# Pre-norm linear-attention block with a matrix layer on one core: the normalisation of x's columns moves from GpSimd to VectorE, and the passage to the second half is reordered

## The chip, the cores and the metric

The kernel runs on one core of one Trainium2 chip. The metric is the device time of the whole program in microseconds, lower is better. The engines are TensorE (PE in the profile; PEld is its loading of weights), VectorE (DVE), ScalarE (ACT), GpSimd (POOL) and SyncE (SP). SP only issues DMAs here; ACT issues some too.

## The reference

```python
def reference(x, Wq, Wk, Wv, Wo, Wa, ba, CB, SCB, bias):   # x: (4, 2048, 512) fp32
    n = layernorm(x)                       # over the 512 columns, eps 1e-5
    q, k, v = n @ Wq, n @ Wk, n @ Wv       # 512 -> 1024 = 16 heads of 64
    q, k = elu(q) + 1, elu(k) + 1
    a = sigmoid(n @ Wa + ba + 2)           # one decay per head and token
    # per head, over the tokens of a sequence:
    #   S = a*S + k v^T,  z = a*z + k,  out = (q S) / (q z + 1e-6)
    x = x + out @ Wo                       # 1024 -> 512
    n2 = layernorm(x)
    return x + (n2 @ CB.T) * (SCB / 127) + bias
```

## The kernel before, in words

The 8192 tokens are cut into NC = 64 chunks of 128. Matrix products are done in three passes (high part by high part, high by low, low by high) of numbers split in two: ScalarE makes the high part with a copy (`..._hi`), VectorE subtracts it for the low part (`..._lo`).

**First half** (`step`, i from -1 to NC + 1, on every engine; chunks are taken two by two, `pair`, with b = i % 2). TensorE makes k and v of a chunk (`unit`, 12 matmuls of 512 columns each) and q of two chunks together (`q_unit`, 24 matmuls of 256 columns), and between these, at the head of each step, the small matmuls of the attention: `transposes` of k, `carried` (q by the state), `delta` (k by v), `within` (scores by v), `scores`. `transposes` waits at its head for VectorE's results of the step before (`M`, `qs`, `S_mid`, the weighted v, all of k and q). The first steps (to 1 on TensorE, to 3 on the others) and the last ones are written out; between them each engine runs a loop.

**x's columns.** The first product needs the normalised x with its 512 columns on the partitions. SP loads a pair's transposed x (`xT_in`, 128 x 4 x 256 numbers). The statistics are per token, so they lie on partitions (`moments`, 128 x 2 chunks x 2), and have to be laid out along the free dimension of all partitions: `store_norm` (L508) writes `moments` to `norm_rows` in HBM, and `spread_norm` (L513) loads it into all 128 partitions of `bias_b`. In the even step GpSimd first makes the inverse deviation for the next pair (L627), waits for `xT_loaded` and `norm_loaded`, and subtracts the mean (L644) and multiplies by the inverse deviation (L648), in four instructions of 128 x 256 each. After this ScalarE (`x_hi`) and VectorE (`x_lo`, L905) split the columns in the odd step. `norm_rows` is [C, 4], so the four numbers of a token are one piece of 16 bytes.

**SP's order** in an even step (L520 to 564): `store_norm`; a wait for TensorE's `num_ready[0]` of the step before; `spread_norm`, which waits until the store has landed; four loads of decays (`abc`, `spread_decays`, L458); `store_rows(1)` (L422, four DMAs); four loads of products (`pbc`, L467); `store_rows(0)`. Every SP instruction waits in this order.

**VectorE's order** in an even step, from `elu_k(1, 0)` on (L1152 to 1190): `elu_k(1)`, `normalised(0)` (den, rden, num_sb, attn), `decay_matrix(1)` (a scan, L1109), `weighted_v(1)` (L1012), `elu_q(2)`, `decay_matrix(0)`, `elu_q(3)`, `elu_k(0)`, `carried_on`. `elu_k(0)` is the last thing for which TensorE's next `transposes` waits; it needs ScalarE's relu and exp of the last k unit.

**Second half** (`step2`): per chunk a product of the attention's rows with Wo (`output_product`, 24 matmuls into DS), `residual` (add x, statistics), the inverse deviation on GpSimd, `residual_normal`, a transpose, the split (`fT_hi`, `fT_lo`), the matrix layer (`ffn_product`, 12 matmuls into NUM), and the sum that is stored.

**The passage** between them: SP loads the matrix layer's weights, `scale` and `bias` (`ffn_weights`, L409), GpSimd multiplies the four weight tiles by `scale` (L655), ScalarE and VectorE split them (`ffn_weights_hi` L692, `ffn_weights_lo` L941). The columns of chunk 0 are turned by TensorE (`turn`, L1566) and split by `turned_hi` (L847) and `turned_lo` (L1210). VectorE ends step NC + 1 with `residual(1)`, `residual_normal(1)`, `rows_lo(3)` and `normalised(1)` of the last chunk, whose transpose waits until the attention rows stored before it have left `attn`; then in step2(1) come `residual(2)` with the bias and the deviation, and `ffn_weights_lo`; in step2(2) `residual_normal(2)`, `turned_lo`, the transpose of chunk 1, `rows_lo(4)` and `residual(3)`; in step2(3) `fT_lo` of chunk 1 and `residual(4)`. TensorE's first `ffn_product` (L1592) waits for all four low weight tiles and for `turned_lo`, behind the output product of chunk 2.

```python
510                     sp.wait_ge(rstd_ready, pairs[1])
511                     sp.dma_start(norm_rows, moments[:, :, :].rearrange("p s a -> p (s a)")).then_inc(norm_stored, 16)
...
515                     sp.wait_ge(norm_stored, p16[0])
516                     wait(sp, xT_normal, pairs[-1])
517                     sp.dma_start(bias_b[:, :], norm_rows.rearrange("(q c) m -> q (c m)", q=1).broadcast_to([128, 4 * C]))\
```

## Time and profile before

| | |
|---|---|
| median of 3 runs | 1965.36 us (1963.75 to 1965.54) |
| the profiled execution, its own time | 1965.75 us |
| its span | 1964.0 us |
| mean granted TensorE clock | 0.998 |
| PE busy | 1939.4 us, 99% |
| DVE busy | 1645.7 us, 84% |
| ACT busy | 687.1 us, 35% |
| POOL busy | 389.6 us, 20% |
| steps of the first half | 24.8 to about 1431 us |
| second half | about 1431 us to the end |

A line of a timeline or a page gives the engine, the line of the kernel (L1109), the operation, the tensor written <- the tensors read, and in brackets the idle time of the engine just before it with what ended it. SPq and ACTq are the issuing of DMAs. "Idle" of an engine other than TensorE costs nothing in itself. 1.75 us of the profiled execution lie outside its span.

### The profile page before, as it was taken

To read this page: it belongs to the slowest core of one execution; us is meant where nothing else is said; L and a number is where in the kernel's file an instruction comes from. 1 tells how busy PE (TensorE), PEld (TensorE's weight loads), DVE (VectorE), ACT (ScalarE), POOL (GpSimd) and SP (SyncE) were. 2 spreads that over 40 slices of the span, in tenths; PEclk is the share of its full clock that TensorE was granted. 3 is DMA by queue.
4 is the path that set the end of the run, shared out by engine and by line. 5 is a ranking of instruction groups with operands and counts; after the bars stand their busy time and mean duration, and the time that the engine had idled before them with its cause. 6 is when DMAs were issued, how large, how long until landed. Compare 5 with 4: busy or idle time off the path is not lost.

```text
span 1964.0 us, 69099 instructions
## 1 busy us (share of the span) xinstructions
PE 1939.4 (99%) x26926; PEld 1690.8 (86%) x26926; DVE 1645.7 (84%) x2918; ACT 687.1 (35%) x1288; POOL 389.6 (20%) x368
## 2 busy tenths in 40 slices
PE   8999999999999999999999999999989999999999
PEld 7888888898888888988888888888878888888887
DVE  8788888888888888888888888888787777777776
ACT  5334334333433343344333433343422222222221
POOL 3222222232222222332222223222010000000000
PEclk9999999999999999999999999999999999999999
DMA  6343443444443444444344444445476666666665
GB/s 217 89 94 96 99 115 94 110 106 104 100 97 98 105 105 108 104 104 105 97 98 102 108 101 107 105 108 128 98 164 163 161 161 161 161 160 160 161 161 117
DMA packets 596067, 237.40 MB, mean 121 GB/s; under 512 B 432064, under 2 KB 546240, under 8 KB 596032
## 3 DMA queue, kind: packets, MB, share of 16 engines
q1 hardware_dynamic: 560896, 204.94, 43.9%
q10 hardware_dynamic: 35136, 32.00, 5.7%
q8 instruction: 21, 0.34, 0.1%
q14 instruction: 14, 0.11, 0.0%
HBM read 168.59 MB, written 51.97 MB: 112 GB/s over the span
## 4 chain that ended last, share of the span: by engine, by line
PE 95%; DVE 2%; issue 1%; DMA 1%; SPq 1%; POOL 0%; ACT 0%; POOLq 0%; DVEq 0%
PE G L1325 54%; PE DS L1283 17%; PE NUM L1283 9%; PE NUM L1394 4%; PE SC L1447 3%; PE DS L1426 3%; PE NUM L1408 3%; PE SC L1273 2%; PE DS L1467 1%; DVE w_lo L912 0%; DMA attn_cols<-attn 0%; SPq L429 0%; DMA norm_rows<-moments 0%; DMA abc<-decay_rows 0%; DVE D L1109 0%
## 5 line engine op out<-in xcount | busy, mean ns | idle before, releaser
L1325 PE MATMUL G<-w_hi,xT_hi 128*128 128x512 f32 x1024 | 406.9, 397 | 0.4 <-DVE w_lo L912 0.4
L1325 PE MATMUL G<-w_lo,xT_hi 128*128 128x512 f32 x1024 | 399.8, 390 | 0.0
L1325 PE MATMUL G<-w_hi,xT_lo 128*128 128x512 f32 x1024 | 398.7, 389 | 0.0
L734 ACT ACTIVATE relu_t<-G 128x512 f32<-128x512 f32 x256 | 153.4, 599 | 451.9 <-PE G L1325 449.9
L1325 PE MATMUL G<-xT_hi,w_hi 128*128 128x256 f32 x1024 | 290.2, 283 | 0.2 <-DVE w_lo L912 0.2
L1325 PE MATMUL G<-xT_lo,w_hi 128*128 128x256 f32 x1024 | 289.8, 283 | 0.0
L1325 PE MATMUL G<-xT_hi,w_lo 128*128 128x256 f32 x1024 | 289.7, 283 | 0.0
L1325 PEld LDWEIGHTS G<-w_hi,xT_hi 128*128 128x128 f32 x1024 | 192.4, 188 | 42.2 <-issue 0.6
L1325 PEld LDWEIGHTS G<-w_hi,xT_lo 128*128 128x128 f32 x1024 | 192.3, 188 | 41.4
L1325 PEld LDWEIGHTS G<-w_lo,xT_hi 128*128 128x128 f32 x1024 | 192.6, 188 | 35.5
L702 ACT ACTIVATE w_hi<-at_rows 128x512 fp32r<-128x512 f32 x128 | 73.8, 624 | 383.7 <-PE DS L1283 365.9
L1325 PEld LDWEIGHTS G<-xT_hi,w_hi 128*128 128x128 f32 x1024 | 196.3, 192 | 3.9 <-DVE w_lo L912 0.7
L1283 PE MATMUL DS<-w_hi 128*128 128x512 f32 x512 | 199.5, 390 | 0.0
L1283 PE MATMUL DS<-w_hi,w_lo 128*128 128x512 f32 x512 | 199.2, 389 | 0.0
L1283 PE MATMUL DS<-w_lo,w_hi 128*128 128x512 f32 x512 | 199.2, 389 | 0.0
L644 POOL TENSOR_TENSOR xT_in<-xT_in,bias_b 128x256 f32<-128x256 f32 x124 | 140.4, 1163 | 295.3 <-DMA bias_b<-norm_rows 295.3
L1325 PEld LDWEIGHTS G<-xT_hi,w_lo 128*128 128x128 f32 x1024 | 196.3, 192 | 2.4
L1325 PEld LDWEIGHTS G<-xT_lo,w_hi 128*128 128x128 f32 x1024 | 196.3, 192 | 0.0
L648 POOL TENSOR_TENSOR xT_in<-xT_in,bias_b 128x256 f32<-128x256 f32 x124 | 182.0, 1495 | 2.4
L1109 DVE TENSOR_TENSOR_SCAN D<-abc,eye 128x512 f32<-128x512 f32 x128 | 175.0, 1367 | 0.5 <-DMA abc<-decay_rows 0.5
L629 POOL TENSOR_TENSOR moments<-vareps,minus_half 128x2 f32<-128x2 f32 x32 | 22.5, 702 | 716.3 <-DVE vareps L894 716.3
L735 ACT ACTIVATE exp_t<-G 128x512 f32<-128x512 f32 x256 | 151.7, 593 | 0.0
(137 smaller groups left out, 3609.0 us busy)
## 6 DMA issues: line engine op xcount, KB each, us to landing
abc<-decay_rows SPq DMA_DIRECT2D x256, 128.0 KB, 3.2
pbc<-product_rows SPq DMA_DIRECT2D x256, 128.0 KB, 3.1
attn_cols<-attn SPq DMA_DIRECT2D x512, 64.0 KB, 2.2
at_rows<-attn_cols ACTq DMA_DIRECT2D x244, 128.0 KB, 2.8
xt<-in_x SPq DMA_DIRECT2D x64, 256.0 KB, 3.1
x_in<-in_x SPq DMA_DIRECT2D x64, 256.0 KB, 3.0
out_rows<-xt SPq DMA_DIRECT2D x64, 256.0 KB, 3.0
xT_in<-in_xT SPq DMA_DIRECT2D x31, 512.0 KB, 4.4
```

Source lines behind the costliest of these rows:

```text
L644: made = pool.tensor_tensor(x4[:, kt, :, :], x4[:, kt, :, :], norm_b[:, 0, :, :], ALU.subtract)
L648: made = pool.tensor_tensor(x4[:, kt, :, :], x4[:, kt, :, :], norm_b[:, 1, :, :], ALU.mult)
L702: act.activation(turned_out(oT_hi[b], r), turned_in(b, r), ACT.Copy).then_inc(oT_hi_ready[r], 1)
L734: act.activation(relu_t[buffer][:, :], bank[:, :], ACT.Relu)
L735: act.activation(exp_t[buffer][:, :], bank[:, :], ACT.Exp).then_inc(ready, 1)
L1109: nc.vector.tensor_tensor_scan(D[:, hs(r), :].rearrange("p h c -> p (h c)"), abc[:, HH * L * r:HH * L * (r + 1)], eye8[:, :, :].rearrange( ...
L1283: made = nc.tensor.matmul(to, a[:, kt, :], w[:, kt, :], start=(kt == 0 and n == 0), stop=(kt == tiles_k - 1 and n == 2))
L1325: made = nc.tensor.matmul(to, lhs, rhs, start=(n == 0), stop=(n == len(passes) - 1))
L1394: made = nc.tensor.matmul(num_of(a, e, j), qs[ps, GH * r + j, L * a:L * a + L], (S_mid if a else S[o])[ps, GH * r + j, :], start=(j == 0), ...
L1408: made = nc.tensor.matmul(num_of(a, e, j), M[ps, r, 2 * j + e, :], v1[o][ps, HH * r + 2 * j + e, :], start=False, stop=(j == GH - 1))
L1426: made = nc.tensor.matmul(DS[64 * e:64 * e + 64, U * a + E * j:U * a + E * j + E], k[ps, DH * h:DH * h + DH], vw[ps, h, :], start=True, st ...
L1447: made = nc.tensor.matmul(SC[64 * a:64 * a + 64, at:at + L], kT[ps, GH * r + j, ts], qT[ps, GH * r + j, C * (b ^ r) + L * a:C * (b ^ r) + ...
```

## The change

- `norm_rows` becomes [4, C]: the means of the even chunk, its inverse deviations, and those of the odd chunk are four runs of 128 numbers. The store writes 512 single numbers of 4 bytes; the load still gives each partition 512 numbers, and `norm_b` is now contiguous in the token.
- `store_norm` stands behind the wait for `num_ready[0]`; `spread_norm` behind the four loads of decays.
- GpSimd's eight instructions per pair are gone (its inverse deviation stays); VectorE does them as two of 128 x 1024: the subtraction ahead of `elu_q(2)`, the multiplication behind `decay_matrix(0)` and ahead of `elu_q(3)`, both in the even step.
- Passage: `turned_hi`/`turned_lo` of chunk 0 move to step2(1), ahead of the weights; the weights' splits are cut into two and two (step2(1) and step2(2)); GpSimd's inverse deviation of chunk 1 goes between the second and the third weight multiplication; TensorE's first `ffn_product` waits for each weight tile by itself; VectorE's `normalised(1)` of the last chunk and SP's `store_rows(1)` of it move to the end of step2(3).

```diff
-    norm_rows = nc.dram_tensor("norm_rows", [C, 4], fp32).ap()
+    norm_rows = nc.dram_tensor("norm_rows", [4, C], fp32).ap()
...
-        norm_b = bias_b[:, :].rearrange("p (c s a) -> p a s c", s=2, a=2)
+        norm_b = bias_b[:, :].rearrange("p (s a c) -> p a s c", s=2, a=2)
+        x_tiles = xT_in[:, :, :].rearrange("p k (s c) -> p k s c", s=2)
...
                 def store_norm():
-                    sp.dma_start(norm_rows, moments[:, :, :].rearrange("p s a -> p (s a)")).then_inc(norm_stored, 16)
+                    sp.dma_start(norm_rows.rearrange("m c -> c m"), moments[:, :, :].rearrange("p s a -> p (s a)"),
+                                 allow_slow_non_contiguous=True).then_inc(norm_stored, 16)
...
                 gates = b == 1 and exists(i + 1)
-                if b == 0 and exists(i + 2):
-                    store_norm()
                 if b == 0 and exists(i):
                     wait(sp, num_ready[0], one[-1])
                 if b == 0 and exists(i + 2):
-                    spread_norm()
+                    store_norm()
                 if exists(i):
                     spread_decays(1, this_pair, b)
                 if b == 0 and exists(i + 1):
                     spread_decays(0, this_pair, 1)
+                if b == 0 and exists(i + 2):
+                    spread_norm()
...
-                if exists(i - 2):
+                if exists(i - 2) and not (isinstance(i, int) and i == NC + 1):
                     store_rows(1, i - 2, one[-2])
...   (SP, end of step2)
+                if isinstance(i, int) and i == 3:
+                    store_rows(1, NC - 1, NC)
...   (GpSimd, step)
-                    inverse_deviation(pairs[1])
-                    pool.wait_ge(xT_loaded, p16[0])
-                    pool.wait_ge(norm_loaded, p16[0])
-                    for kt in range(KT):
-                        made = pool.tensor_tensor(x4[:, kt, :, :], x4[:, kt, :, :], norm_b[:, 0, :, :], ALU.subtract)
-                    made.then_inc(xT_centred, 1)
-                    pool.wait_ge(xT_centred, pairs[0])
-                    for kt in range(KT):
-                        made = pool.tensor_tensor(x4[:, kt, :, :], x4[:, kt, :, :], norm_b[:, 1, :, :], ALU.mult)
-                    made.then_inc(xT_normal, 1)
+                    inverse_deviation(counts(pool, pair, 1, (1,))[1])
                 if isinstance(i, int) and i == NC:
...
                     for kt in range(KT):
+                        if kt == 2:
+                            inverse_deviation2(2)
                         pool.tensor_tensor(raw_wf[kt], raw_wf[kt], scale, ALU.mult).then_inc(wf_scaled, 1)
...   (ScalarE, step2)
-                if isinstance(i, int) and i == 2:
-                    turned_hi(1, 0)
                 if exists(i + 1):
                     rows_hi(r64[1], one[-1], 1 - b)
+                if isinstance(i, int) and i == 2:
+                    ffn_weights_hi(range(2, KT))
...
                 if isinstance(i, int) and i == 1:
-                    ffn_weights_hi()
+                    turned_hi(1, 0)
+                    ffn_weights_hi(range(2))
...   (VectorE, step)
+                def centred_columns():
+                    dve.wait_ge(xT_loaded, x16[0])
+                    dve.wait_ge(norm_loaded, x16[0])
+                    nc.vector.tensor_tensor(x_tiles, x_tiles, over_tiles(0), ALU.subtract).then_inc(xT_centred, 1)
+                def normal_columns():
+                    dve.wait_ge(xT_centred, pairs[0])
+                    nc.vector.tensor_tensor(x_tiles, x_tiles, over_tiles(1), ALU.mult).then_inc(xT_normal, 1)
...
                 elif exists(i + 1):
+                    if exists(i + 2):
+                        centred_columns()
                     elu_q(2, 1)
                     decay_matrix(0)
+                    if exists(i + 2):
+                        normal_columns()
                     elu_q(3, 0)
...   (VectorE, end of step NC + 1)
                     rows_lo(3, 0)
-                    normalised(1)
...   (VectorE, step2)
-                if isinstance(i, int) and i == 2:
-                    turned_lo(1, 0)
...   (behind the transpose of step2)
+                if isinstance(i, int) and i == 2:
+                    ffn_weights_lo(range(2, KT))
...   (end of step2)
-                if isinstance(i, int) and i == 1:
-                    ffn_weights_lo()
+                if opening:
+                    turned_lo(1, 0)
+                    ffn_weights_lo(range(2))
+                if isinstance(i, int) and i == 3:
+                    normalised(1, NC, 64 * (NC - 1))
...   (TensorE, step2)
                 if isinstance(i, int) and i == 2:
-                    pe.wait_ge(wf_lo_ready, KT)
-                if exists(i - 2):
+                    pe.wait_ge(num_copied[1], NC)
+                    pe.wait_ge(fT_lo_ready, 1)
+                    for kt in range(KT):
+                        pe.wait_ge(wf_lo_ready, kt + 1)
+                        made = passes(F[0], (fT_hi[0], fT_lo[0]), (wf_hi, wf_lo), range(kt, kt + 1), KT)
+                    made.then_inc(F_ready, 1)
+                elif exists(i - 2):
```

`over_tiles(a)` is `norm_b[:, a:a + 1, :, :].broadcast_to([128, KT, 2, C])`: the same 256 numbers for each of the four column tiles. `normalised(1)` in steps 2 to NC is the same as before; it only takes its counts as arguments.

## Rows read from the trace of the kernel before

**Rows 1.** The page, part 1, busy time of each engine.
```profile
PE 1939.4 (99%) x26926; PEld 1690.8 (86%) x26926; DVE 1645.7 (84%) x2918; ACT 687.1 (35%) x1288; POOL 389.6 (20%) x368
```
**Rows 2.** Waits of PE: what it waited for, us in total, times, longest.
```profile
PE NUM L1394 <- issue: 6.8, 5, 2.2
...
PE NUM L1283 <- DVE w_lo L1213: 4.4, 1, 4.4
PE SC L1273 <- DVE k L996: 2.0, 1, 2.0
```
**Rows 3.** Windows: busy us (instructions) of each engine, then granted clock, DMA share, GB/s.
```profile
50.00:52.00 2.00, 2.00 (x98) 2.00 (x93) 0.95 (x3) 0.00 (x0) 0.00 (x0) 0.60 0.00 0
...
1452.00:1453.00 1.00, 1.00 (x4) 0.81 (x3) 1.00 (x3) 0.00 (x0) 0.00 (x0) 0.50 0.41 119
```
**Rows 4.** Timeline of DVE in an even step, GpSimd busy from 784.18 on.
```profile
784.53 1.12 DVE L996 SCALAR_TENSOR_TENSOR k<-exp_t,relu_t 128x512 f32<-128x512 f32 x1 [0.15 <-ACT exp_t L735]
...
789.78 1.13 DVE L1012 TENSOR_TENSOR vw<-v,D 128x520 f32<-128x520 f32 x1
...
793.93 1.28 DVE L1003 SCALAR_TENSOR_TENSOR qT<-exp_t,relu_t 128x512 f32<-128x512 f32 x1
795.75 0.69 DVE L996 SCALAR_TENSOR_TENSOR k<-exp_t,relu_t 128x512 f32<-128x512 f32 x1 [0.54 <-ACT exp_t L735]
```
**Rows 5.** Timeline of DVE in the odd step before, same instructions, GpSimd idle.
```profile
766.30 0.69 DVE L996 SCALAR_TENSOR_TENSOR k<-exp_t,relu_t 128x512 f32<-128x512 f32 x1
...
768.77 1.18 DVE L1109 TENSOR_TENSOR_SCAN D<-abc,eye 128x512 f32<-128x512 f32 x1
770.05 0.70 DVE L1012 TENSOR_TENSOR vw<-v,D 128x520 f32<-128x520 f32 x1
```
**Rows 6.** Timeline of SP's DMA issues in the even step of rows 4.
```profile
780.49 0.33 SPq L517 DMA_DIRECT2D bias_b<-norm_rows  x1
781.02 2.62 SPq L463 DMA_DIRECT2D abc<-decay_rows  x4
```
**Rows 7.** DMA issues: tensors, queue, count, KB each, median us to landing.
```profile
bias_b<-norm_rows SPq DMA_DIRECT2D x31, 256.0 KB, 3.2
...
norm_rows<-moments SPq DMA_DIRECT2D x31, 2.0 KB, 2.2
```
**Rows 8.** The row stores of 700 to 900 us by themselves (72 of them).
```profile
DMA to landing us min/median/max: 2.1/2.2/4.3
```
**Rows 9.** Opening, DVE timeline: from the scaled q to the last k.
```profile
37.22 1.31 DVE L1064 TENSOR_TENSOR qs<-qT,pbc 128x512 f32<-128x512 f32 x1
...
45.78 1.34 DVE L996 SCALAR_TENSOR_TENSOR k<-exp_t,relu_t 128x512 f32<-128x512 f32 x1
```
**Rows 10.** Opening and a later step, chain of waits: start us, us, what.
```profile
49.24 1.99 PE SC L1447 x64
...
96.72 1.02 PE SC L1447 x64
```
**Rows 11.** Passage, timeline of DVE.
```profile
1444.65 0.71 DVE L1081 STREAM_TRANSPOSE attn<-num_sb 128x512 f32<-128x512 f32 x1 [3.75 <-DMA attn_cols<-attn]
1445.28 0.65 DVE L958 TENSOR_TENSOR relu_t<-DS,x_in 128x512 f32<-128x512 f32 x1
...
1452.15 1.24 DVE L950 TENSOR_TENSOR w_lo<-at_rows,w_hi 128x512 fp32r<-128x512 f32 x2
...
1459.13 0.70 DVE L1231 TENSOR_TENSOR w_lo<-kT,w_hi 128x512 fp32r<-128x512 f32 x1
```
**Rows 12.** Passage, timeline of POOL.
```profile
1437.41 0.66 POOL L633 TENSOR_TENSOR rstd<-vareps,minus_half 128x1 f32<-128x1 f32 x1 [73.57 <-DVE vareps L970]
1441.39 2.56 POOL L655 TENSOR_TENSOR abc<-abc,eye 128x512 f32<-128x512 f32 x2 [3.32 <-DMA qT<-in_CBT]
```
**Rows 13.** Passage, chain of waits: the first two matrix-layer products.
```profile
1451.35 4.47 PE NUM L1283 x12
...
1461.27 2.72 PE NUM L1283 x12
```

More of the change, by code:

```diff
@@ L1146, in step @@
                     rows_lo(2, 1)
-                    normalised(1)
+                    normalised(1, one[-2], a64[-3])
                 if exists(i):
@@ L1154, in step @@
                 if exists(i - 1) and not last:
-                    normalised(0)
+                    normalised(0, one[-1], a64[-2])
                 if exists(i):
@@ L1159, in step @@
                 if last:
-                    normalised(0)
+                    normalised(0, one[-1], a64[-2])
                 if isinstance(i, int) and i == NC - 2:
```

59 lines of the change are left out of this document (29 added, 30 removed).

## The prediction, made before the changed kernel was run

> **What bounds the kernel now.** Read the page's busy times first: TensorE is busy for 1939.4 of 1964.0 us, VectorE for 84% [rows 1]. So little over 24 us of the span can be won unless TensorE's work changes, and the diff changes none of it. VectorE and GpSimd matter only where TensorE waits for them. The waits of PE come next [rows 2]: 4.4 us once for a low part on VectorE (the first matrix-layer product, in the passage), 2.0 us once for VectorE's k (in the opening), and 6.8 us in five places where it waits for nothing that the profile shows. The change can touch the first two. Third, the granted clock behind them: 0.60 from 50 to 52 us, behind the wait of the opening, and 0.50 behind that of the passage [rows 3], where 1.0 is 2.4 GHz and 0.5 is 1.2 GHz. Each of the two idle stretches is therefore paid twice, once as a wait and once in matmuls at the low clock. Last, the timelines of VectorE, SP and GpSimd, for what the moved work meets.
>
> **Part 1, the normalisation in the steady steps (31 pairs).** Removed are eight GpSimd instructions; no one but ScalarE, VectorE and TensorE in the next step waits for their result, so that alone is worth nothing. What they cost is seen on VectorE. From `elu_k(1)` to the start of `weighted_v(1)` takes 789.78 - 784.53 = 5.25 us with GpSimd busy [rows 4] and 770.05 - 766.30 = 3.75 us in the odd step with GpSimd idle [rows 5]: 1.5 us lost. From there to the end of `elu_q(3)` takes 5.43 us (to 795.21) [rows 4], for which the undisturbed prices are about 0.61 for each 512-column operation and 1.28 for the scan (768.77 to 770.05 [rows 5]), so 0.61 + 0.61 + 1.28 + 0.61 = 3.1: 2.3 us lost. Together some 3.8 us a pair come back.
>
> Beside this row stands a rule of the Trainium skill, "SBUF — State Buffer", the sections on engine ports: a VectorE instruction with two SBUF inputs and a GpSimd instruction that reads SBUF exclude each other for the whole instruction. The rows agree in sign (0.69 against 1.12 us for the same k), not in a full block; the sum goes by the rows.
>
> Added on VectorE are two instructions of 128 x 1024. Nothing of this size is in the trace. It is bounded by two of 512 back to back: 1.24 us for a pair of `rows_lo` [rows 11] and 1.40 for two at the length of `vw` with its start and end [rows 5]. I take 1.22, the spacing of instructions that follow each other, as one long instruction saves one start; so 2.4 us a pair (2.4 to 2.8) come in and 3.8 go out. VectorE then reaches `elu_k(0)` at 784.53 + 3.75 + 0.61 + 1.22 + 0.61 + 1.28 + 1.22 + 0.61 = 793.8, while ScalarE hands the k over only at 795.75, where VectorE already waited 0.54 us before [rows 4]. So 1.9 us of room stand ahead of the instruction on which TensorE depends. The steady steps stay as they are: priced at nothing, hidden behind TensorE's q, k and v matmuls; without this cover 2.4 us a pair, 75 us.
>
> **Part 2, SP's order.** In the even step SP is held by `num_ready[0]` until 780.49 [rows 6]. The store now goes there, then four loads of decays (2.62 us of issuing), then the load, which waits for the store's landing. Behind it wait `store_rows(1)`, the four product loads and `store_rows(0)`. The store has 512 pieces of 4 bytes in place of 128 of 16, which the trace doesn't show. Lower bound: the old store's 2.2 us [rows 7]. Upper bound: the attention row stores, also 512 pieces (of 128 bytes), 2.2 us in the middle and 4.3 at most [rows 8]. I take 3 us, nearer the median of the store with as many pieces, with something for numbers that are single. It lands at 783.5, the load is issued at about 783.9 (held by the issues ahead of it, not by the landing), and lands 3.2 us later [rows 7], at 787.1. VectorE wants it at 784.53 + 3.75 + 0.61 = 788.9. With a store of 4.3 us the load lands at 788.1, still in time. The products are pushed back by one issue, under 0.8 us. ScalarE reads them at the end of the step, several us later. Cost: nothing.
>
> **Part 3, the opening.** VectorE works without a pause from the scaled q at 37.22 to the end of k at 47.12 [rows 9], and TensorE, idle for 2.0 us [rows 2], starts right behind it, so without the wait at about 45.2. New chain: qs 0.62, scan 1.28, vw 0.61, subtraction 1.22, q 0.61, scan 1.28, multiplication 1.22, q 0.61, k 0.69: 8.1 us, end at 45.4. Of the 2.0 us 1.8 come back (1.4 with the dearer instructions). The 64 score matmuls then take 1.02 instead of 1.99 us [rows 10], as the clock has no pause ahead of it: 0.9. The decay loads are issued sooner than before, since they no longer stand behind the landing. Sum 2.7 us (1.5 to 3.0).
>
> **Part 4, the passage.** VectorE stood still for 3.75 us at 1444.65, in `normalised(1)`, until stored rows had left `attn` [rows 11]. All behind it, `residual(2)` at 1445.28 first, started late. That instruction group is now two steps later. `residual(2)` then waits only for TensorE's product of chunk 1, which ended 24 matmuls and a turn ahead of the idle stretch: the stretch began at 1451.35 - 4.4 = 1447.0, 24 matmuls take 5.44 us (12 take 2.72 [rows 13]), a turn 0.5, so about 1441.0. From `residual(2)` to `rows_lo(4)` VectorE needed 1452.15 - 1445.28 = 6.9 us [rows 11], and the new order has the same instructions in it; that gives 1447.9. The weights come later than that: four GpSimd multiplications from 1441.39 at 1.28 us each with the inverse deviation of 0.66 between them [rows 12] end at 1447.2; 0.6 for ScalarE's copy and 0.6 for VectorE's subtraction make 1448.4, and up to 1.3 us more where VectorE and GpSimd meet, as in part 1. So `rows_lo(4)` starts at 1448.4 to 1449.7, against 1452.15. TensorE starts the first matrix-layer product at once at 1447.0, waits a little for the third or fourth tile and then for `rows_lo(4)`, and does the output product of chunk 3 until 1455.1 to 1456.4. The next matrix-layer product needs `fT_lo` of chunk 1, which came 7.0 us behind the start of `rows_lo(4)` (1459.13) [rows 11] and took 0.7: now done at 1456.1 to 1457.4. That product began at 1461.27 [rows 13]. Gain 3.8 to 5.1 us, the clock's part in it (4.47 against 2.72 us for the same 12 matmuls [rows 13]). What is late next is this split of chunk 1, with about 1 us. The moved `normalised(1)`, some 1.8 us of VectorE in the next round, gives back up to 0.5. Sum 4.0 us (3 to 5).
>
> **The sum.** 2.7 + 4.0 = 6.7 us. From the profiled execution's own 1965.75 us (its span and 1.75 outside) that is 1959.05; this execution stands 0.39 above the median 1965.36, which gives 1958.7. I forecast 1959. Its own range is 1956.5 to 1961.5: 4.5 to 8 us from the bounds of parts 3 and 4, with 1 us either way for the five places without a visible cause, whose places hang on code that moves.
>
> A measurement of this kernel can tell about 0.2%, 3.9 us, from no change.
>
> **Rivals.** (a) *The store is slow.* The mechanism is the one of part 2: VectorE waits at `centred_columns`, and everything behind it in the even step with it. The load lands at 780.49 + L + 0.3 + 3.2; VectorE has room until 788.9 + 1.9 = 790.8. It decides from L = 6.8 us on; beyond it each us costs 31 us in all. At L = 8 the time is 1959 + 37 = 1996. Against it: nothing that SP stores lands after more than 4.3 us in rows 8; for it: no row has single numbers of 4 bytes. The Trainium skill, "DMA: Bandwidth & Descriptors", says in its specifications that pieces under 512 bytes are read, modified and written, and in its table of practices that a last dimension that isn't contiguous becomes a piece per element and should be avoided. By this rule 512 pieces cost what they cost for any size under 512 bytes, which is the 2.2 to 4.3 us of rows 8, and the time stays. Chance 0.07.
> (b) *Only one seam pays.* In the passage the freed wait is taken by another: the weights stand behind GpSimd, the rows behind ScalarE's queue, and the clock still falls after two short stops; 1.5 us are left of the 4.0. With the opening's 2.7 this is 4.2, 1961.2. The same result comes if the opening fails (norm not landed by 39.7 there, behind the weight loads) and the passage pays: 1961.4. For it: part 4 has three new near misses; the rows of the opening leave only 0.1 us. Chance 0.2, half of it within 0.2%.
> (c) *Nothing arrives*: VectorE's two instructions take 2 us each, or the waits at the seams are covered by others. Room of 1.9 us in the steady step still holds with 1.6 us more. Then 1965 to 1963. Chance 0.08.
>
> **The numbers.** The forecast has 0.65; (a) 0.07, (b) 0.2, (c) 0.08. The range takes (b) in, up to 1963.5. Faster by over 0.2%: 0.65 and half of (b), 0.76; within 0.2%: half of (b) and most of (c), 0.16; slower 0.08.
>
> **What would show it.** VectorE's instructions in even steps all at their short lengths, with two of 1.2 us at `centred_columns` and `normal_columns` and no wait for `bias_b<-norm_rows` ahead of them; an idle time of over 1 us ahead of `elu_k(0)`; the norm store landing in about 3 us; no wait of PE for k near 45 us and clock 1.0 behind it; in the passage no wait of over 1.5 us, and clock 1.0. A mean of over 1.5 us for the two new instructions, a store over 5 us, or a wait of PE at each even step's end would make the prediction wrong.

## The result and the profile after

The changed kernel takes **2187.16 us** (median of 5 runs, 2184.27 to 2190.91) against 1965.54 us of the kernel before on the same chip (5 runs): ratio 1.1123, 95% interval 1.1111 to 1.1135. The prediction said 1959.0 us and 1956.5 to 1963.5; it is wrong by 228 us and in its sign. The profiled execution took 2184.27 us, its span is 2182.4 us, the mean granted clock 0.953.

First the page of the changed kernel: parts 1 and 4, and one group of part 5 (compare [rows 1]).

```profile
PE 2001.1 (92%) x26926; PEld 1749.2 (80%) x26926; DVE 1595.9 (73%) x2980; ACT 685.8 (31%) x1288; POOL 67.7 (3%) x120
...
PE 65%; DMA 20%; DVE 8%; issue 5%; SPq 2%; POOL 0%; DVEq 0%; ACT 0%; POOLq 0%; ACTq 0%
...
L1119 DVE TENSOR_TENSOR_SCAN D<-abc,eye 128x512 f32<-128x512 f32 x128 | 155.0, 1211 | 239.5 <-DMA abc<-decay_rows 239.5
```

TensorE was busy for 99% of the span and is now for 92%. VectorE has less to do than before (1595.9 against 1645.7 us), though it took over GpSimd's work: the short durations of part 1 came. But 239.5 us of its idle time stand ahead of one instruction, the scan that turns the loaded decays into the decay matrix.

The waits (what an engine waited for, us in total, times, longest), where [rows 2] had 2.0 us once for k:

```profile
DVE D L1119 <- DMA abc<-decay_rows: 239.5, 31, 9.1
...
PE SC L1289 <- DVE k L1009: 161.6, 31, 6.3
...
DVE xT_in L1088 <- DMA bias_b<-norm_rows: 5.4, 3, 3.4
```

In each of the 31 pairs VectorE waits 7.7 us for decays, the last k of the step comes late by it, and TensorE waits 5.2 us for that k. The instruction that reads the stored norm (L1088) waits almost nowhere: by the time the decays are in, so is it.

One pair in order of time. SP's issues (compare [rows 6]), VectorE (compare [rows 4]) and TensorE's first matmul behind the wait:

```profile
748.01 0.42 SPq L512 DMA_DIRECT2D norm_rows<-moments  x1
748.65 2.63 SPq L464 DMA_DIRECT2D abc<-decay_rows  x4
758.47 0.34 SPq L519 DMA_DIRECT2D bias_b<-norm_rows  x1
```
```profile
763.66 1.22 DVE L1119 TENSOR_TENSOR_SCAN D<-abc,eye 128x512 f32<-128x512 f32 x1 [9.06 <-DMA abc<-decay_rows]
764.98 0.70 DVE L1025 TENSOR_TENSOR vw<-v,D 128x520 f32<-128x520 f32 x1
765.59 1.22 DVE L1088 TENSOR_TENSOR xT_in<-xT_in,bias_b 128x1024 f32<-128x1024 f32 x1
...
768.46 1.20 DVE L1093 TENSOR_TENSOR xT_in<-xT_in,bias_b 128x1024 f32<-128x1024 f32 x1
...
771.11 1.12 PE L1289 MATMUL SC<-ident,k 64*128 64x64 f32 x16 [6.27 <-DVE k L1009]
```

The load of the norm waits for nothing but the landing of the store, so the store took 758.47 - 748.01 = 10.5 us [rows 7 had 2.2]. The chain of waits shows 14.2 us in one decay load, from 749.42 to 763.64. What the transfer engines did meanwhile stands in the last two columns of the windows (busy us and instructions of each engine, granted clock, DMA share, GB/s):

```profile
749.00:751.00 2.00, 2.00 (x11) 1.65 (x10) 1.93 (x5) 0.07 (x1) 0.00 (x0) 1.00 0.12 1
751.00:753.00 2.00, 2.00 (x11) 1.65 (x9) 1.81 (x5) 1.02 (x2) 0.00 (x0) 1.00 0.00 0
753.00:755.00 2.00, 2.00 (x16) 1.92 (x15) 1.46 (x3) 0.60 (x1) 0.00 (x0) 1.00 0.13 12
755.00:757.00 2.00, 2.00 (x19) 2.00 (x18) 0.00 (x0) 0.47 (x1) 0.00 (x0) 1.00 0.15 7
757.00:759.00 2.00, 2.00 (x19) 2.00 (x18) 0.00 (x0) 0.61 (x2) 0.00 (x0) 1.00 0.16 5
759.00:761.00 2.00, 2.00 (x12) 1.71 (x11) 0.00 (x0) 1.09 (x2) 0.00 (x0) 1.00 0.47 19
761.00:763.00 2.00, 2.00 (x10) 1.65 (x10) 0.00 (x0) 0.00 (x0) 0.00 (x0) 1.00 0.94 204
...
772.00:774.00 2.00, 2.00 (x73) 1.88 (x73) 0.16 (x1) 1.08 (x2) 0.00 (x0) 0.50 0.67 127
774.00:776.00 2.00, 2.00 (x116) 2.00 (x112) 1.54 (x5) 0.93 (x2) 0.00 (x0) 0.79 0.72 266
```

Four loads of decays are issued, and for 10 us hardly anything moves: 0 to 12 GB/s. The store lands at 758.5; the stretch behind it still has 19 GB/s, the next one 204. The two last lines are the second price: behind the 6.27 us of waiting TensorE goes on at 1.2 GHz (0.50) until about 774.8, nearly 4 us of work.

The queue of these DMAs in three stretches (packets, MB, and the time that the packets took, as a share of 16 engines' time): 748 to 750 us, 753 to 760, and 761 to 763.

```profile
q1 hardware_dynamic: 528, 0.00, 12.6%
...
q1 hardware_dynamic: 29, 0.05, 14.0%
...
q1 hardware_dynamic: 238, 0.41, 94.0%
```

The 512 single numbers are in the first line, 8 ns to a packet, and by 749.4 us the transfer engines were done with them, though the store landed only at 758.5. In the second stretch a packet takes 0.54 us in the mean, behind the landing 0.13. So the hold isn't work of the transfer engines: it shows as packets that take four times as long, and as few of them.

The account closes. Waits for k: 161.6 us. TensorE's busy time: 2001.1, against 1938.1 in the run below that has the old store and everything else of the change, 63.0 us more for the same instructions, the clock's part (2.0 us a pair, the half of those 4). That run waits 1.4 us for k in its opening. Together 161.6 - 1.4 + 63.0 = 223.2 us, and the spans differ by 2182.4 - 1959.3 = 223.1 us.

### The profile page after: what moved, and what is told of

It is laid out like the page before. It is cut to its first block, busy times and chain, and to the rows that moved or that the text cites. A ratio compares the mean times of both kernels' runs of the same rounds, so it can differ in the third digit from the quotient of the medians.

```text
span 2182.4 us, 68943 instructions
## 1 busy us (share of the span) xinstructions
PE 2001.1 (92%) x26926; PEld 1749.2 (80%) x26926; DVE 1595.9 (73%) x2980; ACT 685.8 (31%) x1288; POOL 67.7 (3%) x120
## 2 busy tenths in 40 slices
DMA packets 607970, 237.39 MB, mean 109 GB/s; under 512 B 443968, under 2 KB 558144, under 8 KB 607936
## 4 chain that ended last, share of the span: by engine, by line
PE 65%; DMA 20%; DVE 8%; issue 5%; SPq 2%; POOL 0%; DVEq 0%; ACT 0%; POOLq 0%; ACTq 0%
PE G L1341 24%; DMA abc<-decay_rows 17%; PE DS L1299 15%; PE NUM L1299 8%; PE NUM L1410 4%; PE SC L1463 3%; PE DS L1442 3%; PE NUM L1424 3%; DVE D L1119 3%; PE SC L1289 3%; DMA norm_rows<-moments 2%; DVE qT L1016 1%; SPq L464 1%; DVE k L1009 1%; DVE xT_in L1088 1%
## 5 line engine op out<-in xcount | busy, mean ns | idle before, releaser
L1119 DVE TENSOR_TENSOR_SCAN D<-abc,eye 128x512 f32<-128x512 f32 x128 | 155.0, 1211 | 239.5 <-DMA abc<-decay_rows 239.5
L1289 PE MATMUL SC<-ident,k 64*128 64x64 f32 x1040 | 59.1, 270 | 162.5 <-DVE k L1009 161.6
L1289 PEld LDWEIGHTS SC<-ident,k 64*128 64x128 f32 x1040 | 49.3, 175 | 187.4 <-issue 187.4
L717 ACT ACTIVATE num_sb<-NUM 128x520 f32<-128x520 f32 x128 | 77.4, 605 | 195.8 <-PE NUM L1424 192.1
```

Source lines behind the costliest of these rows:

```text
L717: act.activation(num_sb[r][:, :, :, :], num_banks, ACT.Copy).then_inc(num_copied[r], 1)
L1119: nc.vector.tensor_tensor_scan(D[:, hs(r), :].rearrange("p h c -> p (h c)"), abc[:, HH * L * r:HH * L * (r + 1)], eye8[:, :, :].rearrange( ...
L1289: turned.append(nc.tensor.transpose(to[a][:, L * j:L * j + L], rows[ps, 128 * j:128 * j + 128], ident[ps, ps]))
```

## The experiments

**First round: which part.** The edit of the first run, against the changed kernel: only the layout in memory is taken back.

```diff
-    norm_rows = nc.dram_tensor("norm_rows", [4, C], fp32).ap()
+    norm_rows = nc.dram_tensor("norm_rows", [C, 4], fp32).ap()
...
-        norm_b = bias_b[:, :].rearrange("p (s a c) -> p a s c", s=2, a=2)
+        norm_b = bias_b[:, :].rearrange("p (c s a) -> p a s c", s=2, a=2)
...
-                    sp.dma_start(norm_rows.rearrange("m c -> c m"), moments[:, :, :].rearrange("p s a -> p (s a)"),
-                                 allow_slow_non_contiguous=True).then_inc(norm_stored, 16)
+                    sp.dma_start(norm_rows, moments[:, :, :].rearrange("p s a -> p (s a)")).then_inc(norm_stored, 16)
...
-                    sp.dma_start(bias_b[:, :], norm_rows.rearrange("(q m) c -> q (m c)", q=1).broadcast_to([128, 4 * C]))\
+                    sp.dma_start(bias_b[:, :], norm_rows.rearrange("(q c) m -> q (c m)", q=1).broadcast_to([128, 4 * C]))\
```


> The changed kernel with norm_rows back at [C, 4] (128 pieces of 16 bytes, as before), all else as changed: VectorE normalises, the store stands behind num_ready, the passage is reordered. Theory T (the 512 single numbers take about 10 us to land and hold the decay loads issued right behind them; VectorE's scan waits, then TensorE): the loss is gone, about 1959 us, no wait of VectorE's scan for abc, no wait of TensorE at the end of even steps. Rival R1 (VectorE's two long instructions make it late in every pair): 2100 us or more remain. Rival R2 (it is the new place of the store and the load in SP's order): most of the loss remains, over 2000 us.

Measured: 1961.16 us (11 runs, 1959.63 to 1964.89) against 1965.01; ratio 0.998, interval 0.9971 to 0.9989. Repeated later on another chip:

> The run with the old layout again, beside the one with contiguous reads, so that the two and the kernel before are timed on one chip: 1961.2 us, 3.5 to 4 us below the kernel before.

Measured: 1961.52 us against 1966.06, ratio 0.9981 (0.9972 to 0.999). So the layout in memory is the whole loss; the rest of the change gains 4 to 4.5 us. The price of this layout is in VectorE's reads, which step over 16 bytes (compare 1.22 and 1.20 above):

```profile
785.46 2.05 DVE L1087 TENSOR_TENSOR xT_in<-xT_in,bias_b 128x1024 f32<-128x1024 f32 x1
...
789.17 1.97 DVE L1092 TENSOR_TENSOR xT_in<-xT_in,bias_b 128x1024 f32<-128x1024 f32 x1
```

The second run is the kernel before with nothing but the new layout (store, load and GpSimd's view of it, as in the change).

```diff
-    norm_rows = nc.dram_tensor("norm_rows", [C, 4], fp32).ap()
+    norm_rows = nc.dram_tensor("norm_rows", [4, C], fp32).ap()
...
```


> The kernel before with only norm_rows as [4, C] and the store of 512 single numbers; GpSimd normalises, SP's old order (store, wait for num_ready, load behind the landing, then the decay loads). Theory T: the store is issued about 4 us ahead of the old place of the load and lands about 10 us after its issue, near 787 in the clock of rows 6, so the decay loads are issued about 6 us later than now and land about 790.5 where VectorE's scan wants them at 788.5; GpSimd's stretch moves 6 us later too and still disturbs VectorE. 2 to 4 us a pair, 2030 to 2090 us. R1 and R2, by which the layout is innocent: 1965 us.

Measured: 2195.61 us (2 runs), ratio 1.1171 (1.115 to 1.1191): a loss as large, where I expected about half of it. The number missed because the loss takes another way. The waits of this kernel, and one of them in TensorE's timeline:

```profile
PE DS L1427 <- issue: 57.2, 24, 5.8
PE NUM L1395 <- issue: 33.8, 25, 5.0
PE NUM L1409 <- issue: 26.5, 7, 6.8
```
```profile
760.97 0.27 PE L1395 MATMUL NUM<-S_mid,qs 64*64 64x65 f32 x1 [5.01 <-issue]
```

Here the store goes out at 753.28, while TensorE is in its hundreds of small matmuls, and TensorE stands still in the middle of a row of equal ones, with no operand missing that the profile shows. The three rows make 117.5 us; 14.0 more (6 waits, 4.1 us at most) lie between the long matmuls of k, v and q (L1326), so these aren't spared. One might think of instructions that are held in memory like the loads. The trace doesn't bear it out: the page has 35 packets on its instruction queues, and none of them between 190 and 1580 us, where nearly all these stops lie. What holds TensorE there is open.

The next run puts the changed kernel's store back to its early place in SP's order.

```diff
+                if b == 0 and exists(i + 2):
+                    store_norm()
                 if b == 0 and exists(i):
                     wait(sp, num_ready[0], one[-1])
-                if b == 0 and exists(i + 2):
-                    store_norm()
```


> The changed kernel with only the store of the 512 numbers back at its old place in SP's order, ahead of the wait for num_ready (about 4 us sooner); the decay loads follow it as in the changed kernel. Theory T: of the about 10 us some 4 have passed when the decay loads are issued, so VectorE's scan waits 3 to 5 us in place of 7.7 and TensorE 0.5 to 2.5 us a pair in place of 5.2; 1975 to 2080 us. R1: as the changed kernel, 2187.

Measured: 2178.69 us (2 runs), ratio 1.1084 (1.1064 to 1.1105); the expected range missed again.

```profile
PE NUM L1410 <- issue: 48.0, 33, 4.6
PE DS L1442 <- issue: 45.7, 17, 5.5
PE NUM L1424 <- issue: 31.0, 9, 5.4
...
DVE D L1119 <- DMA abc<-decay_rows: 2.0, 2, 1.1
```

The decays are in time now (2.0 us in all), and the loss is where it was in the second run: 124.7 us without a visible cause in these three rows. So the change's new place for the store, behind `num_ready`, took the hold away from TensorE's small matmuls, and put it on the decay loads. Moving it further back is the next case:

```diff
-                if b == 0 and exists(i + 2):
-                    store_norm()
                 if exists(i):
                     spread_decays(1, this_pair, b)
                 if b == 0 and exists(i + 1):
                     spread_decays(0, this_pair, 1)
                 if b == 0 and exists(i + 2):
+                    store_norm()
                     spread_norm()
```


> The changed kernel, with the store of the 512 single numbers behind the two pairs of decay loads in place of ahead of them. My theory (everything that goes to memory is held for some 10 us from the store on): the decays are in or nearly so before the hold, the wait of VectorE for them falls from 7.7 us to under 2 us, and the wait goes to the centring: the load of the norm is issued some 10 us after the store, near 14 us behind num_ready, lands 3 us later, and VectorE, which wants it 8.4 us behind num_ready and has 1.9 us of room, waits about 8 us a pair. TensorE loses 5 to 7 us a pair with its clock: 2110 to 2200 us. The rival, that only transfers queued directly behind the store suffer: the decays come in time, the store lands in 3 to 4 us, 1960 to 1975 us.

Measured: 2132.59 us, ratio 1.0854 (1.083 to 1.0878), within the range.

```profile
776.20 0.58 SPq L512 DMA_DIRECT2D norm_rows<-moments  x1
783.96 0.34 SPq L519 DMA_DIRECT2D bias_b<-norm_rows  x1
...
788.25 1.23 DVE L1087 TENSOR_TENSOR xT_in<-xT_in,bias_b 128x1024 f32<-128x1024 f32 x1 [6.38 <-DMA bias_b<-norm_rows]
```

No wait for decays is left; VectorE waits 197.9 us in 31 times for the norm. This is rival (a) as the prediction drew it, with a landing of 7.8 us in this place. None of the three places in SP's order makes the store harmless.

**The passage by itself**: the kernel before with the change's order of splits, residual, weights and row stores between the two halves, and nothing of the rest.

```diff
-                if exists(i - 2):
+                if exists(i - 2) and not (isinstance(i, int) and i == NC + 1):
                     store_rows(1, i - 2, one[-2])
...
                     for kt in range(KT):
+                        if kt == 2:
+                            inverse_deviation2(2)
                         pool.tensor_tensor(raw_wf[kt], raw_wf[kt], scale, ALU.mult).then_inc(wf_scaled, 1)
...
-                    ffn_weights_hi()
+                    turned_hi(1, 0)
+                    ffn_weights_hi(range(2))
```


> The kernel before with only the passage reordered (splits and residual ahead of the weights, the last chunk's normalisation and its stores later). By the prediction's part 4: 4.0 us less (3 to 5), about 1961.4 us, no idle time of TensorE over 1.5 us in the passage, clock 1.0 there. If another wait takes the place: under 2 us.

Measured: 1963.46 us (11 runs), ratio 0.9992 (0.9983 to 1.0001), 1.5 us less by the medians, where 4.0 was expected; the interval takes in no change at all. How much the passage itself gains is worked out from the traces in the next section.

**Second round: what about the store is slow.** These runs keep the harmless store (the first run above is their base) and add a second one that nobody reads, right behind it in SP's order and in its 31 places. So the hold is seen at the decays, which follow it; VectorE's wait for them is only what the hold takes beyond the room they have.

```diff
+    probe = nc.dram_tensor("probe", [NC // 2, 4 * C], fp32).ap()
...
                     store_norm()
+                    sp.dma_start(probe[bass.ds(at, 1), :].rearrange("o (m c) -> (o c) m", c=C), ident[:, 0:4], allow_slow_non_contiguous=True).then_inc(probed, 16)
```


> e1_old_layout (1961 us) with one more DMA per pair behind the norm store: 512 single numbers of the constant `ident` to a scratch tensor in HBM, lying side by side as in the changed kernel, [4, C]; nobody waits for it. Theory T (the store itself occupies what the DMAs behind it need, for about 10 us): the decay loads behind it land late as in the changed kernel, 2150 to 2200 us. Rival R3 (only the wait of the norm load for the landing costs, a store that nobody waits for is free): 1961 to 1965 us.

Measured: 2133.5 us (2 runs), ratio 1.0867 (1.083 to 1.0903), somewhat below the range and far from the rival's.

```profile
774.42 0.41 SPq L531 DMA_DIRECT2D probe<-ident  x1
...
784.68 1.22 DVE L1124 TENSOR_TENSOR_SCAN D<-abc,eye 128x512 f32<-128x512 f32 x1 [4.19 <-DMA abc<-decay_rows]
```

The loss comes with a store that holds nothing back by a semaphore: the traffic is enough. The next run changes only the addresses, 64 bytes from number to number:

```diff
-    probe = nc.dram_tensor("probe", [NC // 2, 4 * C], fp32).ap()
+    probe = nc.dram_tensor("probe", [NC // 2, 4 * C * 16], fp32).ap()
-probe[bass.ds(at, 1), :].rearrange("o (m c) -> (o c) m", c=C)
+probe[bass.ds(at, 1), :].rearrange("o (m c z) -> (o c) m z", c=C, z=16)[:, :, 0]
```


> As p1_512_adjacent, but each of the 512 single numbers goes to its own line of 64 bytes (a step of 16 numbers). If the cost is per single number, wherever it lies (T1): as p1, 2150 to 2200 us. If it is that neighbours in one line are written by several DMA engines at once and queue for the line (T2): near 1961 us, at most 1980.

Measured: 1962.12 us, ratio 0.9991 (0.9979 to 1.0002). The same 512 pieces of 4 bytes cost nothing that can be told from noise. They were not cut or joined in another way: both pages count 612434 packets and 237.46 MB. The view of the instructions that write `probe` gives the landing:

```profile
DMA to landing us min/median/max: 2.0/3.1/4.8
```

And from another queue (the first form of the store, issued by ScalarE in the same step):

> As p1_512_adjacent, but issued from ScalarE's DMA queue, at the same point of the step (behind num_ready[0]); the decay loads stay in SP's queue. If only the order within a queue delays what is behind the store (T3): near 1961 us. If the store blocks what all queues share, on the way to HBM or in it (T4, which TensorE's stops in the middle of a batch in e2 and e4 speak for): 2100 us or more.

Measured: 2120.13 us (2 runs), ratio 1.0798 (1.0767 to 1.083).

```profile
DVE D L1128 <- DMA abc<-decay_rows: 138.9, 31, 10.3
```

The decays, on SP's queue, are held by a store on ScalarE's. It isn't the order in a queue.

**Third round: number and spacing.** The form of the edit stays; only the shape of `probe`, its view and the part of `ident` change. In the order of the runs below, the part of the line with the destination's view and the source:

```diff
+.rearrange("o (c m) -> (o c) m", c=C), ident[:, 0:1]
+.rearrange("o (t z) -> (o t) z", z=16)[:, 0:8], ident[:, 0:1]
+.rearrange("o (j t) -> (o t) j", t=16), ident[:, 0:1]
+.rearrange("o (m c z) -> (o c) m z", c=C, z=16), ident[:, 0:64].rearrange("p (m z) -> p m z", m=4)
+.rearrange("o (c m) -> (o c) m", c=16), ident[0:16, 0:1]
+.rearrange("o (m c z) -> (o c) m z", c=C, z=2)[:, :, 0], ident[:, 0:4]
+.rearrange("o (m c z) -> (o c) m z", c=C, z=4)[:, :, 0], ident[:, 0:4]
+.rearrange("o (c m) -> (o c) m", c=64), ident[0:64, 0:1]
```

> As p1_512_adjacent, but only 128 single numbers, side by side (one per token). If the cost goes with the number of pieces: a quarter of about 10 us, 2.5 us, which e1's room in the even step covers nearly: 1961 to 1985 us. If it is a fixed price of any store of single numbers: 2150 us or more.

> As the run with 128 single numbers side by side, but only eight neighbours stand in one 64-byte stretch of memory (16 stretches, each filled to a half). Theory A (the cost goes by how many single numbers fall into the same 64 bytes): the hold is about half of the 10 us there, some 5 us, so that VectorE's wait for the decays falls from 7.9 us to about 3 us and the time to 1970 to 2010 us. Theory B (the cost goes by the number of single numbers, wherever they lie): 128 were no cheaper than 512, so there would be no change from 2086 us. Theory C (it needs partners from many transfer engines in one stretch; here the eight may well come from one): free, 1961 to 1965 us.

> The same 128 single numbers and the same 512 bytes of memory as the run side by side, sixteen to a 64-byte stretch, but token c at place (c mod 8) * 16 + c div 8, so that the sixteen of a stretch come from tokens eight apart. Theory A (number of single writes into the same 64 bytes): the same time, 2060 to 2110 us, decays waited for some 8 us. Theory C (which engines meet in a stretch decides): it goes up or down by more than 20 us from 2086.

> The extra store has 512 pieces again, in the same place of SP's order, but each is 64 bytes long and fills its stretch of memory alone, 32 kB in all. Theory A: no stretch is shared, so it is free, 1961 to 1966 us, landing in 3 to 4 us. Theory B' (many small pieces of under 512 bytes are slow by themselves): as with the 512 single numbers side by side, over 2100 us.

> The extra store has only 16 single numbers, side by side in one 64-byte stretch. Theory A' (the writes of one stretch are taken one after the other, and the stretches of a store side by side with each other): one stretch with sixteen writers holds as long as eight or thirty-two of them do, so it lands in 6 to 10 us, and if the hold is everybody's, VectorE waits for the decays and the time is 2000 to 2080 us. Theory B'' (it takes many colliding writes in all): under 4 us of landing and 1961 to 1966 us.

> The extra store of 512 single numbers with 8 bytes from one to the next, so that eight stand in each 64-byte stretch; side by side (sixteen in each) it cost 10 us of hold and 168 us in all, 64 bytes apart nothing. If the hold goes by the writers of a stretch: about half, 4 to 7 us until it lands, a wait of 2 to 4 us a pair for the decays, 1985 to 2045 us. If it needs numbers that touch each other (no gap between them): free, 1961 to 1966 us. If it goes by the number of pieces: over 2100 us.

> The same with 16 bytes from one to the next, four in each 64-byte stretch. By writers of a stretch: landing in 3 to 4.5 us, 1961 to 1975 us. By number of pieces: over 2100 us.

> 64 single numbers side by side, four full stretches. 16 of them in one stretch cost nothing that could be seen, 128 in eight stretches 9 us of hold, 512 in thirty-two 10 us. If the hold grows with the number of colliding writes up to a bound of 10 us, 64 hold about half of what 128 do: 3 to 6 us, 1963 to 2020 us. If there is a threshold between 64 and 128 (all transfer engines must have several of them): 1961 to 1965 us.

| store beside the harmless one | numbers in a 64-byte stretch | ratio to before (interval) | waits for decays, us (times) | landing, median us |
|---|---|---|---|---|
| none | - | 0.998 (0.9971 to 0.9989) | none | - |
| 512 numbers, step 4 bytes | 16 | 1.0867 (1.083 to 1.0903) | 149.0 (32) | not resolved |
| 512, step 8 | 8 | 1.0092 (1.0076 to 1.0109) | 36.7 (15) | 4.3 |
| 512, step 16 | 4 | 1.001 (1.0001 to 1.002) | 24.1 (27) | 3.7 |
| 512, step 64 | 1 | 0.9991 (0.9979 to 1.0002) | 3.4 (6) | 3.1 |
| 512 pieces of 64 bytes | full | 0.9987 (0.9977 to 0.9998) | none | 2.8 |
| 128 numbers, step 4 | 16 | 1.0624 (1.0589 to 1.0659) | 115.2 (32) | not resolved |
| 64 numbers, step 4 | 16 | 1.041 (1.0392 to 1.0427) | 81.2 (32) | 6.9 |
| 16 numbers, step 4 | 16, one stretch | 0.9985 (0.9976 to 0.9994) | 0.7 (1) | 1.3 |
| 128 numbers, order scattered | 16 | 1.0466 (1.0438 to 1.0493) | 91.6 (32) | 7.4 |
| 128 numbers, groups of 8 | 8 | 1.0094 (1.007 to 1.0118) | 27.1 (10) | 3.5 |

The waits at the two ends of the spacing series, as they stand in the profiles (step 4, then step 64):

```profile
DVE D L1124 <- DMA abc<-decay_rows: 149.0, 32, 9.9
PE SC L1294 <- DVE k L1014: 130.3, 31, 8.6
```
```profile
PE NUM L1415 <- issue: 6.0, 5, 1.5
DVE D L1124 <- DMA abc<-decay_rows: 3.4, 6, 1.2
PE SC L1294 <- DVE k L1014: 1.4, 1, 1.4
```

What follows. (1) It isn't the number of pieces: 512 of them cost between nothing and 171 us (2133.5 - 1962.1, on one chip) by their addresses alone. (2) It isn't their size: single numbers of 4 bytes, each in a stretch of its own, cost no more than 64-byte pieces. (3) At a fixed number the cost falls steeply with the distance between neighbours: 149.0, 36.7, 24.1, 3.4 us of waiting. It isn't that neighbours touch: 128 numbers in groups of eight touch within their groups and cause 27.1 us of waiting, the 128 side by side 115.2. (4) At a fixed distance it grows with the number, by a leap from 16 to 64 (0.7 to 81.2 us, landing after 1.3 and 6.9 us) and from there far less than in proportion: 115.2 for 128, 149.0 for 512. The theory that sixteen writers of one stretch set the hold, whatever else is there, falls with the 16 numbers, which cost nothing. (5) Which token stands beside which matters a little: the scattered order has the same count of numbers and stretches as the 128 side by side, and 23.6 us less of waiting. No view tells which transfer engine writes which number. So that a stretch is written by several of them, and not by one, stays beside the count of writers as what may decide: at eight or fewer to a stretch, they may all come from one.

By what was expected: the 128 side by side (2085.89, 2 runs) hit neither guess, far dearer than a quarter and cheaper than a fixed price. The times of the half-filled stretches, the 64-byte pieces and the step of 16 came out as the writers of a stretch would have it, the step of 8 just below its range (1982.57 against 1985). But VectorE's wait with the half-filled stretches is 0.9 us a pair, where about 3 were said, and 1.2 with the step of 8, where 2 to 4 were said. The scattered order (2054.74) is 5 us below the range of that theory and over 20 us from the run side by side, as the rival wanted. The 16 numbers went against it, and the 64 (2046.2) were dearer than either guess. So the plain theory (writers per stretch) is half of the truth: many single writes must fall into shared stretches at once. What makes everything wait meanwhile stays open; the stretch of 64 bytes is the step at which I measured no cost, not a size that a run has proved.

**The price of the strided reads.** The first run's kernel, with the loaded numbers read as rows:

```diff
-        norm_b = bias_b[:, :].rearrange("p (c s a) -> p a s c", s=2, a=2)
+        norm_b = bias_b[:, :].rearrange("p (s a c) -> p a s c", s=2, a=2)
```


> As the changed kernel with the old [C, 4] layout in memory, but VectorE reads the loaded numbers as if they were laid out in rows, so that means and deviations are mixed up and the result is not x normalised; the work and the traffic are those of the run with the old layout. It gives the price of the long strides by themselves. Both VectorE instructions take 1.22 us in place of 2.05 and 1.96; in the steady steps that is hidden (nothing), in the opening 1.6 us less work ahead of k: 0.8 to 1.6 us, more with the clock. 1959 to 1961 us against 1961.2; if it stays at 1961 or above, the opening ends at another wait.

Measured: 1959.5 us (5 runs, 1958.58 to 1959.86), ratio 0.9966 (0.9952 to 0.9979), 2.0 us below the run with strides beside it. In effect this is the work that the prediction priced, with a store as cheap as it assumed: 1959.5 against its 1959.0. It isn't a kernel that can be used. Of those that can, the best measured is the first run: the change with its old [C, 4] layout, 1961.2 to 1961.5 us, below both kernels.

## Why the prediction was wrong, point by point

**Part 2, the store: the step that failed.** "I take 3 us, nearer the median of the store with as many pieces" and "Cost: nothing". It lands after 10.5 us. The lower bound held; the upper one (4.3 us, from row stores with as many pieces, of 128 bytes) compared the wrong property. Those pieces fill their stretches of memory; the new ones share them sixteen at a time, which no row of the trace before shows. The text called them "numbers that are single" and took the row nearest by count. The range therefore had a bound that was no bound: nothing excluded a larger value.

A second error stood behind it. The part looked for the effect of a slow store only at its reader, `centred_columns`. In the changed kernel the four decay loads behind it are hit first, at `decay_matrix(1)`, as the hold is everybody's. At the measured 10.5 us the formula of rival (a) gives 1959 + 31 x (10.5 - 6.8) = 2074 us; the real place and the clock behind each wait made it 2187.

**Rival (a)** had the cause, the threshold (6.8 us) and a chance of 0.07. Where the decays are issued first, its mechanism is what happens. The Trainium skill, "DMA: Bandwidth & Descriptors", has in its section "Specifications" that pieces under 512 bytes are read, modified and written; the prediction took from it that they all cost alike. No run here shows such reads, and the runs speak against that reading: pieces of 4 bytes at a step of 64 landed in 3.1 us, and at a step of 4 held everything for 10. Its section "Rules for kernel authors" has that a last dimension that isn't contiguous becomes a piece per element and should be rearranged. On the pieces the trace agrees: 607970 packets against the 596066 of the run with the old layout, 384 more for each of 31 stores. As a warning it pointed the right way here, and the prediction left it, though the store with a step of 64 has as many such pieces and is free.

**Part 1, steady steps: right.** Prices: 1.22 and 1.20 us for the two instructions (1.22 said). VectorE's qT fell from a mean of 966 to 689 ns with GpSimd idle. Room ahead of `elu_k(0)`: 1.9 us said; 2.05 in the run with contiguous reads and the harmless store,

```profile
791.16 0.69 DVE L1008 SCALAR_TENSOR_TENSOR k<-exp_t,relu_t 128x512 f32<-128x512 f32 x1 [2.05 <-ACT exp_t L728]
```

and 0.58 us with the strided reads in the same place, so those are hidden too, as rival (c) had it.

**Part 3, the opening: right in the same run.** Predicted: the wait of TensorE goes, its matmuls start at 45.2 in place of 47.26, the 64 score matmuls take about half. Measured with contiguous reads:

```profile
44.96 0.71 PE L1288 MATMUL SC<-ident,k 64*128 64x64 f32 x16
...
46.95 1.16 PE L1462 MATMUL SC<-qT,kT 64*64 64x64 f32 x64 [0.65 <-ACT kT L709]
```

2.3 us sooner and 1.16 for 1.99 us [rows 10], 3.1 us in all, for 2.7. With one reservation: the kernel with the passage alone still waits 2.2 us there, and its 64 matmuls took 1.16 us as well, without the half clock. So the clock's 0.8 us is not safely this part's gain. With strided reads the start is at 46.62. In the changed kernel itself nothing of this came: the store of the opening took 9.5 us, VectorE waited 1.4 us for decays and 3.4 for the norm, and TensorE

```profile
50.07 1.12 PE L1289 MATMUL SC<-ident,k 64*128 64x64 f32 x16 [4.78 <-DVE k L1009]
```

**Part 4, the passage: right in kind, mis-sized.** From the last small product before it (the eight matmuls at 1440.84 of the kernel before) to the end of the span there are 523.2 us before, 520.4 with the passage alone (1959.7 - 1439.32) and 520.4 with contiguous reads (1957.7 - 1437.25): 2.8 us in both, where 4.0 (3 to 5) was said. The whole gain of the first is 1.5 us by the medians and 4.3 by these spans, which is the spread of single executions; the 2.8 are read from one execution each. The mechanism came as told: TensorE begins the first matrix-layer product at once, without the 4.4 us wait and the low clock behind it. What is late next:

```profile
PE NUM L1298 <- DVE w_lo L938: 1.6, 1, 1.6
...
PE NUM L1298 <- DVE w_lo L1243: 0.8, 1, 0.8
```

The second line is the "about 1 us" for chunk 1's split. The first is the mis-sized term. For the place where VectorE and GpSimd meet the prediction had "up to 1.3 us more", and its 5.1 us of gain had nothing for it:

```profile
1440.80 2.38 DVE L938 TENSOR_TENSOR w_lo<-abc,w_hi 128x512 fp32r<-128x512 f32 x2
1443.10 1.51 DVE L993 TENSOR_SCALAR k<-relu_t,moments,rstd 128x512 f32<-128x512 f32 x1
...
1445.65 1.25 DVE L938 TENSOR_TENSOR w_lo<-qT,w_hi 128x512 fp32r<-128x512 f32 x2
```

2.38 us for what takes 1.25 five us later, and 1.51 for an instruction of 0.55: 2.1 us more, on the way to the third tile, and GpSimd's row of the same execution covers just that time (3.44 us for what took 2.56 [rows 12]):

```profile
1440.88 3.44 POOL L648 TENSOR_TENSOR qT<-qT,eye 128x512 f32<-128x512 f32 x2
```

With 2.1 us in this place the prediction's own sum gives 5.1 - 2.1 = 3.0 us, and 2.5 to 3.0 with its "up to 0.5" for `normalised(1)`, where 2.8 was measured. The contention that part 1 removes from the steady steps came back in the passage.

**The sum.** Where parts 1, 3 and 4 can be seen without the store they give -6.6 us by the medians (1966.06 - 1959.5), for -6.7. By parts, in the profiled executions, it is 3.1 in the opening (2.7 said), 2.8 in the passage (4.0 said) and 0.5 between them, which is in the reach of the places without a visible cause. So the sum is better than its terms: the opening gave more than said and the passage less, and that they made up for each other is luck. What made the number wrong by 228 us is one store of 2 kB, 31 times.

**Slips in the numbers.** The forecast's 0.65 and half of (b) make 0.75, not 0.76. The bounds, 4.5 to 8 us with 1 us either way, give 1956.4 to 1961.9 from the median, not 1956.5 to 1961.5. Neither bears on the outcome.

## What to carry to other kernels

Price a DMA whose pieces are new in kind by the addresses it writes, not by the count of its pieces: 64 and more single numbers that are neighbours in memory, as a transposing store makes them, were a hazard to everything else in flight, and the same 512 as 16-byte pieces were harmless. When no row of the trace bounds a cost from above, say so, and give the case a chance that fits an unbounded cost, above all when one pass of the loop carries it 31 times. And look for the damage of a slow transfer at every other transfer of that stretch, not at its reader alone.

## What the runs showed of the hardware

- A store of 512 single numbers of 4 bytes side by side held nearly all traffic for 10 us (0 to 12 GB/s against 204 behind it), loads on another queue too (138.9 us of waiting in 31 times). The transfer engines were done with its numbers 1.4 us after the issue. At steps of 8, 16 and 64 bytes the same store cost 21, 5 and about 1 us in all, by the medians against 1961.2, taken on other chips; the last can't be told from noise.
- It needs company: 16 such numbers in one 64-byte stretch were free and landed after 1.3 us, 64 in four landed after 6.9 and cost 81.2 us of waiting in 32 times.
- During the hold TensorE stood still inside rows of small matmuls for 5 us at a time, with no operand missing that the profile shows (117.5 us in three rows of the second run), and now and then between long ones (14.0 us in 6 waits there). Why is open; no packet of the instruction queues lies in that time.
- VectorE's 128 x 1024 subtraction takes 1.22 us with its second operand contiguous and 2.05 with steps of 16 bytes.
- VectorE beside GpSimd: 1.13 us more for a pair of subtractions of 1.25, 0.96 more for a `TENSOR_SCALAR` of 0.55.
